# Relative values of an attention kernel: 128-column table weights against 32-column probability weights on four column tiles

## What is computed

```python
scores = einsum('bhld,bhrd->bhlr', Q, K) * scale + einsum('bhld,lrd->bhlr', Q, rel_k)
attn = softmax(scores, axis=-1)
out = einsum('bhlr,bhrd->bhld', attn, V) + einsum('bhlr,lrd->bhld', attn, rel_v)
return out.transpose(0, 2, 1, 3).reshape(B, L, D) @ Wo.T + bo
```

## Time and profile before

| | |
|---|---|
| median of three runs | 3597.58 us |
| the profiled execution, its own time | 3588.57 us |
| its span | 3586.8 us |
| mean granted TensorE clock | 0.945 |
| busy share PE, PEld, DVE, ACT, POOL | 92, 73, 76, 73, 61% |
| relative values on TensorE (L999) | 27648 loads, 27648 matmuls |
| picks (L1014) | 1024 loads, 1024 matmuls |
| moved by DMA | 701 MB, mean 196 GB/s |

### The profile page before, as it was taken

One profiled execution on the slowest core, in us unless ns is written; L12 is line 12 of the kernel. 1 busy time (PEld: TensorE's weight loads), 2 busy tenths in 40 slices (PEclk: granted clock), 3 DMA queues, 4 the chain that ended last, 5 costly groups with the idle time before them and its releaser, 6 DMA issues. The chain is left out here.

```text
span 3586.8 us, 166713 instructions
## 1 busy us (share of the span) xinstructions
PE 3292.6 (92%) x65430; PEld 2603.2 (73%) x65430; DVE 2736.0 (76%) x7853; ACT 2629.0 (73%) x5852; POOL 2195.9 (61%) x2407
## 2 busy tenths in 40 slices
PE   7599999999999999999999999999999996999990
PEld 4367777777777777777777777777777775579980
DVE  6488888888888888888888888888888886534443
ACT  3288888888888888888888888888888884334440
POOL 0167777777777777777777777777777764810006
PEclk9779999999999999999999999999999998579995
DMA  6766666666666666666666666666666664722124
GB/s 211 231 215 212 211 211 214 215 210 208 212 212 214 213 214 212 210 211 211 212 210 209 212 211 210 212 212 215 212 209 211 215 208 142 270 71 65 61 63 143
DMA packets 356377, 701.33 MB, mean 196 GB/s; under 512 B 59545, under 2 KB 168706, under 8 KB 355346
## 3 DMA queue, kind: packets, MB, share of 16 engines
q1 hardware_dynamic: 349458, 673.92, 58.1%
q0 software_dynamic: 6144, 16.79, 1.4%
HBM read 343.02 MB, written 347.46 MB: 193 GB/s over the span
## 5 line engine op out<-in xcount | busy, mean ns | idle before, releaser
L851 POOL TENSOR_TENSOR pt_near<-pt_full,pt_near 128x512 f16<-128x512 f32 (+3 forms) x1984 | 1839.4, 956 | 780.2 <-DVE pt_near L1156 779.5
L1063 ACT ACTIVATE pt_full<-pb,exp_bias 128x512 f32<-128x512 f32 x2048 | 1316.1, 694 | 437.3 <-PE pb L946 395.0
L1136 DVE TENSOR_REDUCE part_max<-pb 128x1 f32<-128x512 f32 (+3 forms) x1376 | 770.0, 573 | 155.4 <-PE pb L904 153.7
L999 PE MATMUL pb<-pt_near,table_high 128*128 128x64 f16 (+6 forms) x18432 | 833.7, 187 | 0.9 <-DVE rel_out L1189 0.8
L1132 DVE CUSTOM_DVE_ANT_0 near_sum<-pb,skewed 128x512 bf16<-128x512 f32 (+3 forms) x1216 | 675.2, 571 | 200.6 <-PE pb L904 175.4
L999 PE MATMUL pb<-pt_near,table_low 128*128 128x64 f16 (+6 forms) x9216 | 818.2, 187 | 0.0
L999 PEld LDWEIGHTS pb<-pt_near,table_high 128*128 128x128 f16 x18432 | 790.5, 97 | 1.1 <-DVE rel_out L1189 0.9
L999 PEld LDWEIGHTS pb<-pt_near,table_low 128*128 128x128 f16 x9216 | 772.7, 97 | 0.0
L938 PE MATMUL pb<-ident,skewed 128*128 128x128 f32 x3840 | 648.4, 287 | 48.9 <-ACT pt_full L1063 39.1
L972 PEld LDWEIGHTS pb<-v_head,pt_near 128*128 128x128 f16 x13440 | 432.2, 96 | 188.0 <-POOL pt_near L851 97.4
L972 PE MATMUL pb<-v_head,pt_near 128*128 128x33 f16 x13440 | 514.7, 178 | 13.9 <-POOL pt_near L851 7.0
(11 more groups left out here) (183 smaller groups left out, 4102.0 us busy)
## 6 DMA issues: line engine op xcount, KB each, us to landing
skewed<-rel_scratch SPq DMA_DIRECT2D x256, 576.0 KB, 5.5
rel_scratch<-rel SPq DMA_DIRECT2D x416, 319.5 KB, 3.4
rel_scratch<-rel SPq DMA_DIRECT2D x320, 320.0 KB, 2.8
skewed<-rel_scratch SPq DMA_DIRECT2D x64, 512.0 KB, 4.7
skewed<-rel_scratch SPq DMA_DIRECT2D x64, 448.0 KB, 4.3
k_stack<-planes_scratch SPq DMA_DIRECT2D x192, 96.0 KB, 4.9
planes_scratch<-planes SPq DMA_DIRECT2D x64, 256.0 KB, 2.3
rel_scratch<-rel SPq DMA_DIRECT2D x64, 256.0 KB, 2.7
```

Of the source, the lines that this page charges most:

```text
L851: ins = nc.gpsimd.tensor_tensor(pt_piece(c, 1, a, z, near), pt_full[e][:, (a - 4 * g) * P:(z - 4 * g) * P], pt_piece(c, 0, a, z, near), AL ...
L999: ins = nc.tensor.matmul(acc[:, c0:c1, :], keep[table][:, w:w + P], pt_near[half][:, part, c0:c1, d - M_LO, a * SHIFTS:(a + 1) * SHIFTS], ...
L1063: nc.scalar.activation(pt_full[e][:, :], x_ps[e % 2][:, :], ACT.Exp, bias=exp_bias[:, 0:1]).then_inc(s_exp, 1)
L1136: ins = nc.vector.tensor_reduce(best, src, axis=AX.X, op=ALU.max)
```

## The change

The operands change places. The weights are now probabilities: for query offset q0 the columns q0, q0+32, q0+64 and q0+96 of each valid unit, 4 x up to 8 = up to 32 columns, single fp16 elements 64 bytes apart (`SHIFT_STEP` = 32). What moves is the table: 4 shifts x 16 dimensions = 64 columns, in runs of 16 elements. The output has 32 partitions, so four such products, for four successive q0, write the four column tiles of the array (partitions 0, 32, 64, 96). Each step does 4 offsets x 9 distances x 3 products = 108 pairs; where the table has a seam, a product is split in two. One PSUM bank takes the half. To make valid units a prefix, the units of the first half are kept in reverse order (`row_of`), and `pt_near` is indexed by half, part, distance, unit and query.

Mask, pick matrix and the pick matmuls go. VectorE copies the bank to `rel_raw` (one copy a half), SyncE stores it to HBM (256 KB) and, a step later, issues four transfers that read the right shift of each query back into `rel_sum` (16 KB each, pieces of 64 bytes). GpSimd adds and divides behind its low parts. The picks are now 22 steps behind (the store), 23 (the reads) and 25 (the output). `project` makes neither mask nor pick matrix; `mix` takes the units in their new order.

```diff
-SHIFTS = P // DK
-SHIFT_GROUPS = P // SHIFTS
+SHIFTS = 4
+SHIFT_STEP = P // SHIFTS
+COL_TILES = 4
+COL_TILE = P // COL_TILES
+RV_ROW = SHIFTS * P + DK
-LAG_SEL = LAG_RV + HALF_C
-LAG_O = LAG_SEL + 1
+LAG_SEL = LAG_RV + HALF_C + 1
+LAG_O = LAG_SEL + 3
+def table_windows(d, q0):
+    cols = [table_column(d, q0 + SHIFT_STEP * (SHIFTS - 1 - s)) for s in range(SHIFTS)]
+    cut = next((s for s in range(1, SHIFTS) if cols[s] != cols[s - 1] + SHIFT_STEP), SHIFTS)
+    return [(a, z, cols[a]) for a, z in ((0, cut), (cut, SHIFTS)) if a < z]
+def row_of(c):
+    return HALF_C - 1 - c if c < HALF_C else c - HALF_C
-        pt_near = [sb(f"pt_near{i}", [P, 2, HALF_C, REL_BLOCKS, P], FP16) for i in range(2)]
+        pt_near = [sb(f"pt_near{i}", [P, 2, REL_BLOCKS, HALF_C, P], FP16) for i in range(2)]
@@ SyncE, step(it, k) @@
+                if i == 0 and h >= 0 and exists(it, h * HALF_C):
+                    sp.wait_ge(s_rle, h + 1)
+                    if h >= 2:
+                        sp.wait_ge(s_rr[h % 2], 16 * COL_TILES * (h // 2))
+                    sp.dma_start(hbm["rel_values"][h % 2, :, 0:CH], rel_raw[h % 2][:, :]).then_inc(s_rw[h % 2], 16)
+                if i == 1 and h >= 0 and exists(it, h * HALF_C):
+                    sp.wait_ge(s_rw[h % 2], 16 * (h // 2 + 1))
+                    if h >= 2:
+                        sp.wait_ge(s_o, h - 1)
+                    for tile in range(COL_TILES):
+                        sp.dma_start(rel_sum[h % 2][tile:P:COL_TILES, :, :],
+                                     picked_src(h % 2, tile)).then_inc(s_rr[h % 2], 16)
@@ GpSimd @@
+            def output(it, h):
+                pool.wait_ge(s_rr[h % 2], 16 * COL_TILES * (h // 2 + 1))
+                pool.wait_ge(s_or, h + 1)
...
+                nc.gpsimd.tensor_tensor(out[h % 2][:, :, :], rel_sum[h % 2][:, :, :], o_sum[h % 2][:, :, :],
+                                        ALU.add).then_inc(s_o1, 1)
+                pool.wait_ge(s_o1, h + 1)
+                nc.gpsimd.tensor_tensor(out[h % 2][:, :, :], out[h % 2][:, :, :],
+                                        inv_sum[h % 2][:, :, :].to_broadcast([P, HALF_C, DK]), ALU.mult).then_inc(s_o, 1)
@@ TensorE @@
-                        ins = nc.tensor.matmul(
-                            acc[:, c0:c1, :], keep[table][:, w:w + P],
-                            pt_near[half][:, part, c0:c1, d - M_LO, a * SHIFTS:(a + 1) * SHIFTS],
-                            start=(a % HALF_C == 0 and d == 0 and n == 0), stop=(a % HALF_C == HALF_C - 1 and d == M_LO and n == 2))
+                for d in (0, 1, -1, -2, 2, -3, -4, -5, -6):
+                    n_rows = half_rows(half, d)
+                    for n, (name, part) in enumerate((("table_high", 0), ("table_high", 1), ("table_low", 0))):
+                        table = keep[name][:, :].rearrange("p (n d) -> p n d", d=DK)
+                        probs = pt_near[half][:, part, d - M_LO, :, :].rearrange("p c l -> p (c l)")
+                        for tile in range(COL_TILES):
+                            q0 = COL_TILES * j + tile
+                            acc = r_ps[tile * COL_TILE:tile * COL_TILE + n_rows * SHIFTS,
+                                       j * SHIFTS * DK:(j + 1) * SHIFTS * DK].rearrange("p (s d) -> p s d", s=SHIFTS)
+                            for a, z, col in table_windows(d, q0):
+                                ins = nc.tensor.matmul(
+                                    acc[:, a:z, :], probs[:, q0:n_rows * P:SHIFT_STEP],
+                                    table[:, col:col + (z - a - 1) * SHIFT_STEP + 1:SHIFT_STEP, :],
+                                    start=(j == 0 and d == 0 and n == 0), stop=(j == HALF_C - 1 and d == M_LO and n == 2))
@@ VectorE: mask_values and output go @@
+            def rel_values_out(it, h):
+                dve.wait_ge(s_rl, h + 1)
+                if h >= 2:
+                    dve.wait_ge(s_rw[h % 2], 16 * (h // 2))
+                nc.vector.tensor_copy(rel_raw[h % 2][:, :], r_ps[:, :]).then_inc(s_rle, 1)
```

More of the change, by code:

```diff
@@ L101, with table_column @@
 TABLE_ROWS = 10 * P
-def table_window(d, a):
-    j = P * d - SHIFTS * (a + 1) + 1
-    if d == M_LO or (d == M_LO + 1 and a == SHIFT_GROUPS - 1):
+def table_column(d, q):
+    j = P * d - q
+    if d == M_LO or (d == M_LO + 1 and q == P - 1):
         return j - LEFT0
@@ L168, in pieces, with half_rows @@
     return out
-def half_range(half, d):
-    cs = [c for c in range(half * HALF_C, (half + 1) * HALF_C) if 0 <= c + d < NB]
-    return cs[0] - half * HALF_C, cs[-1] + 1 - half * HALF_C
+def row_of(c):
+    return HALF_C - 1 - c if c < HALF_C else c - HALF_C
+def half_rows(half, d):
+    rows = sorted(row_of(c) for c in range(half * HALF_C, (half + 1) * HALF_C) if 0 <= c + d < NB)
+    assert rows == list(range(len(rows)))
+    return len(rows)
 def segments(c):
@@ L360, in _ @@
         def _(pool):
-            ident, pick, shift_mask = keep["ident"], keep["pick"], keep["shift_mask"]
+            ident = keep["ident"]
             nc.gpsimd.memset(keep["blank"][:, :], 0.0).then_inc(s_id, 1)
@@ L620, in attend @@
         s_rle = sem("b_rel_values_on_chip")
-        s_sel = sem("b_rel_values_picked")
+        s_rw = [sem(f"b_rel_values_stored{i}") for i in range(2)]
+        s_rr = [sem(f"b_rel_values_picked{i}") for i in range(2)]
         s_o1 = sem("b_out_steps")
@@ L626, in attend, with picked_src @@
         HALF_STEP = STEP // HALF_C
+        def picked_src(slot, tile):
+            return bass.AP(hbm["rel_values"].tensor, (slot * P + tile * COL_TILE) * RV_ROW + (SHIFTS - 1) * DK,
+                           [[SHIFTS * DK, COL_TILE], [SHIFTS * RV_ROW, HALF_C], [1, DK]])
         def skew_src(slot, width):
@@ L860, in step @@
                         low_part(it, u, e)
+                h, j = half_at(k, LAG_O)
+                if j == 0 and h >= 0 and exists(it, h * HALF_C):
+                    output(it, h)
                 if V0 <= k % NB < V0 + len(V_STAGES) // 2 and exists(it, (k // NB + 1) * NB):
@@ L1006, in pick_values @@
-            def pick_values(it, h, i):
-                if i == 0:
-                    pe.wait_ge(s_rle, it * (2 * HALF_STEP) + 2 * h + 2)
-                    if h:
-                        pe.wait_ge(s_o, it * HALF_STEP + h)
-                ins = nc.tensor.matmul(s_ps[:, i * DK:(i + 1) * DK],
-                                       rel_out[:, i, :, :].rearrange("p a b -> p (a b)"), keep["pick"][:, :],
-                                       start=True, stop=True)
-                if i == HALF_C - 1:
-                    ins.then_inc(s_sel, 1)
+                if j == 0:
+                    if h:
+                        pe.wait_ge(s_rle, h)
+                    u = h * HALF_C + HALF_C - 1
+                    wait_low(pe, it, u, E - 2)
+                    wait_low(pe, it, u, E - 1)
@@ L1020, in step @@
+                if j == HALF_C - 1:
+                    ins.then_inc(s_rl, 1)
             def step(it, k):
@@ L1036, in step @@
                 if rel_on:
-                    for quarter in range(4):
-                        rel_values(it, h, j, quarter)
-                h, j = half_at(k, LAG_SEL)
-                if h >= 0 and j == 0 and exists(it, h * HALF_C):
-                    for i in range(HALF_C):
-                        pick_values(it, h, i)
+                    rel_values(it, h, j)
             pipeline(pe, step)
@@ L1070, in high_part @@
                 for a, z, near in pieces(c, g):
-                    ins = nc.scalar.copy(pt_piece(c, 0, a, z, near), pt_full[e][:, (a - 4 * g) * P:(z - 4 * g) * P])
+                    ins = nc.scalar.copy(pt_piece(c, 0, a, z, near), full_piece(e, g, a, z))
                 ins.then_inc(s_ha, 1)
@@ L1214, in step @@
                 adding, turning = exists(it, a), exists(it, t)
-                h, j = half_at(k, LAG_O)
-                if j == 0 and h >= 0 and exists(it, h * HALF_C):
-                    output(it, h)
                 h, j = half_at(k, LAG_PV + HALF_C)
@@ L1357, in token_rows @@
         def token_rows(n):
-            return rows[:, :, n, :]
+            return rows[:, :, n // HALF_C * HALF_C + row_of(n % NB), :]
         @block.sync
@@ L1836, in program @@
             keep["table_low"] = sbi("table_low", [P, TABLE_N * DK], FP16)
-            keep["pick"] = sbi("pick_dim", [P, DK])
             keep["blank"] = sbi("blank", [CLEAR, D])
-            keep["shift_mask"] = sbi("shift_mask", [P, SHIFTS])
             keep["rv_lo"] = sbi("rv_lo", [P, DK])
```

109 lines of the change are left out of this document (31 added, 78 removed).

## The result

The changed kernel takes 4146.07 us (median of 4 runs, 4122.23 to 4158.21) where the kernel before takes 3597.78 (4 runs, 3597.44 to 3604.18): 1.1511 times as long, 95% interval 1.1455 to 1.1567. It is slower by 548 us. I had forecast 3334 and a gain. The profiled execution took 4158.21 us.

A forecast was written before the change was run, and what follows sets the result against it. TensorE was taken as the bound: 1.70 us a step removed, 1.04 added. The chain then limits the step to 4.95 us, 0.53 less over 512 steps (271 us), plus 7 us at the end: 3334 us, range 3255 to 4250.

The forecast's parts named there:

- What bounds the kernel: Attention stage, 512 steps of 5.48 us: TensorE is the bound, busy 96%; the other engines have 15% of slack.
- What is removed: TensorE's block of 54 pairs, 1.48 us, and the fp32 picks, 0.22 us: 1.70 us a step removed.
- The cost of a group: New block on TensorE: four side-by-side pairs take 31 ns, 27.1 groups a step, 0.84 us.
- rival B: New block: tiles run together, but a load costs twice or does not hide; 47 to 52 ns a group, 3525 us; chance 0.22.
- A: The predicted case: groups of 28 to 33 ns, 3334 us, own range 3257 to 3436; chance 0.38.
- Rival C: New block: loads or pairs go one after another, 4250 us; chance 0.31 with its halfway case (3750 to 4250).
- The layout changes: Before and after the new block on TensorE: two changes of array layout, 0.10 us each, 0.20 us a step.
- The supply of instructions: New block on TensorE: supplying eight instructions a group adds 3 ns; too slow arrival would make the prediction wrong.
- The clock: Attention stage: granted clock 0.99 explains nothing; a fall below that would make the prediction wrong as a whole.
- The DMA part: Store and reads of the relative values stay hidden: GpSimd's output waits for nothing, SyncE still waits for score rows each step.
- The other engines: VectorE 0.16 us a step less, ScalarE unchanged at 4.66, GpSimd at most 1.6 us more in each eighth step.
- What is late next: After the change, a chain from step start through GpSimd's low parts limits the step to 4.92 us, taken as 4.95.

The follow-up runs named there:

- e5: The kernel before with its sixteen recorded pick matmuls replaced by a single one, so the relative values are missing: 3475 us.
- e1: The changed kernel with packed weights, each product loading 32 neighbouring fp16 elements instead of 32 lying 64 bytes apart: 4159 us.
- e4: The changed kernel with the same 108 pairs a step in two blocks, behind the values of the first and second pair of chunks: 4035 us.
- e2: The changed kernel with two column tiles of 64 packed weights and 128 moving columns instead of four tiles, 54 pairs a step: 3590 us.
- e7: The kernel before with 110 single-column weight loads added behind each block of relative values: 4489 us.
- e6: The changed kernel with its 256 KB store and four reads replaced by one 64 KB store and one 64 KB read in 512-byte pieces: 4098 us.
- e11: The changed kernel with packed weights and without the third product (high probabilities by the table's low part), 72 pairs a step: 3546 us.
- e10: The kernel before without the product with the table's low half and with its picks in float16: 3333 us.

## Why the prediction was wrong

**What bounds the kernel: right.** Taking 0.22 us a step off TensorE gave 127 us (e5), so it did set the step.

**What is removed: right.** 1.70 us a step, of which the picks' 0.22 is measured by e5 (0.21 us a step).

**The cost of a group: mis-sized, 31 ns for 53.** I took 31 ns for it because its nearest row was that of row tiles, and those rows are contiguous. The scattered weights make it about 60 ns for 32 columns (e1: 30 ns when packed) and 53 in the mean. That is rival B by its mechanism, and its price of 47 to 52 ns is 1 ns short. The blocks agree: 1.42 and 1.79 us in the two kinds of halves, less 0.15 us to the next line, are 54 ns a group. The same working gives (0.98 - 0.12) / 27.1 = 32 ns for e1, so 31 was right for packed weights. I had named the 64-byte distance, and gave B 0.22. B's time, 3525 us, missed as A's did, because B too left the instructions at next to nothing. Column tiles do run side by side: the members of a group start 5 ns apart in the median. Rival C was wrong in its mechanism, although its price of 4250 us lies nearest to the result; the time agrees by accident, and so does the range, whose upper end is C's price.

**The layout changes: right.** From the last start of the values to the block it is 107 ns, from the block's last start to the transposes 152 in the median (121 in e1 at the least), each 25 before: 0.21 us a step in all, 0.20 forecast.

**The supply of instructions: the step that failed.** In the prediction it is "the 3 ns above it are for supplying eight instructions in that time, which no row shows". I priced it at 3 ns a group, 0.08 us a step; it cost 0.94. My closing line named it as something that would make the whole wrong, but I gave it no rival, no price and no chance. A look at the trace of before would have shown that the question was open: its 8.55 MB of instructions come in 522 pieces, the closest of the stage 3.65 us apart. The forecast asked for 350 instructions in 4.95 us, a piece each 3.6 us on average, closer than any two pieces of that stage. A rival was there to be worked out: 350 instructions are 1.37 pieces, so at 3.65 us a piece the step is at least 5.0 us. More it could not say. The median spacing of 5.73 us was TensorE's own pace and no limit, for there was next to no stop, and that 217 of the instructions stand in one burst (e4) doesn't show in a mean. So the 6.60 us could not have been worked out from the trace of before, but a rival slower than 4.95 us could.

**The clock** was the other thing named as a way to be wrong, and it did fall, to 0.92. e2 brings it back to 1.00 with the stops removed, and e1 takes it down to 0.86 with more of them, so here it goes with the stops; not with them alone, since in e7 it is 0.92 with few stops, where 1.33 us of each step are loads without a matmul. What it costs by itself I can't separate: without the stops, the changed kernel's step is still 5.66 us, where 53 ns a group give 27.1 x 53 + 200 = 1.64 us in place of 1.70, a step of 5.44. The 0.22 us left over are the clock, stops shorter than 0.4 us, or both.

**The DMA part: right.** Output on GpSimd waits for the picked values twice, 30.5 us in all; SyncE still waits for the score rows. These are the waits of the changed kernel, where the last row answers the earlier trace rows:

```profile
POOL out L893 <- DMA rel_sum<-rel_values_scratch: 30.5, 2, 23.5
...
SPq L771 <- ACT rel L1078: 1911.3, 495, 10.2
```

The picked values land in 3.2 us in the median (4.5 taken), but the four reads keep SyncE for 614 ns each in place of 370, which stays hidden. What I had missed is that hidden transfers can still cost: e6 gets 48 us back, nearly all of it from the stops.

**The other engines: right in size.** The new copy takes 692 ns (683 taken), the two operations on GpSimd 455 and 402 ns, and the conversion became faster rather than slower with the new layout, 444 ns for 508. The rows are those of groups by line and shape, and they answer:

```profile
L1179 DVE CAST pt_near<-pt_full 128x512 f16<-128x512 f32 x768 | 314.8, 444 | 16.2 <-PE pb L1015 15.5 <-ACT pt_full L1086 0.5
...
L1207 DVE COPY rel_raw<-pb 128x512 f32<-128x512 f32 x64 | 44.3, 692 | 65.1 <-PE pb L1041 64.9
```

**What is late next: right as far as it was tried.** No kernel went under the chain's 4.92 us: e11 stands at 4.92 us without its stops, e10 at 5.01, both with waits of TensorE for GpSimd's low parts. No run shortens the chain itself, so that it is the limit is argued from these waits, not shown.

## What to carry to other kernels

Cutting a matmul into smaller pieces that run side by side saves array time and spends instructions. Before such a change, count TensorE's instructions in a step, loads too, and set them beside the spacing of the instruction fetches in the trace. In this kernel some 240 in 5.5 us were free, 276 cost 0.4 us of stops and 348 cost 0.9, and of a saving on the array that needed them nothing was left. Look for the saving first where instructions fall with it: a product that can go, or an fp32 product that float16 can do, gave 182 and 117 us without any of the new machinery.

## What the runs showed of the hardware

- TensorE stands still for up to 5.0 us (e1; 4.4 in the changed kernel) when it has used up a piece of 256 instructions before the next has come. The fetches start 3.3 us apart at the closest in the stage, in every kernel with many instructions (3.29 to 3.38), and 4.5 to 5.2 us in the median. Each starts only after TensorE is in the piece before, 1.70 us in the median in the changed kernel, and 2.49 us more pass until a stop ends. Why it starts no sooner was not found: it isn't the trips of the change (e6).
- Four column tiles of 32 weights with 64 moving columns take 30 ns when the weights lie side by side, and 60 when each is a 2-byte element 64 bytes from the next. The scattered groups take 29 ns up to 12 columns and from 20 on some 1.9 ns for each column (39, 47, 53 and 60 ns for 20, 24, 28 and 32). Two column tiles of 64 packed weights with 128 moving take 56 ns (e2).
- A load of a single weight column starts every 12 ns, 110 in 1.33 us, though the profile shows 79 ns for one.
